# A small first transfer, constants made later, turned copies on VectorE, and a new order on all engines

## The reference

```python
x = x + tanh(g_xattn[0]) * _L0_xattn_ref(_layernorm(x), ctx, ctx, mask, ...)   # A0: 16 heads of 8, softmax attention
x = x + tanh(g_ffn[0])   * _L0_ffn_ref(_layernorm(x), ...)                     # M0: 8 experts (top 2) and 2 shared
x = x + tanh(g_xattn[1]) * _L1_xattn_ref(_layernorm(x), ctx, ctx, mask1, ...)  # A1: 16 heads of 8, with biases
x = x + tanh(g_ffn[1])   * _L1_ffn_ref(_layernorm(x), ...)                     # SW: switched attention, 16 heads of 64
x = x + tanh(g_xattn[2]) * _L2_xattn_ref(_layernorm(x), ctx, ctx, ...)         # ML: mLSTM, 4 heads of 32
x = x + tanh(g_ffn[2])   * _L2_ffn_ref(_layernorm(x), ...)                     # CF: quantised layers around a convolution
x = x + tanh(g_xattn[3]) * _L3_xattn_ref(_layernorm(x), ctx, ctx, ...)         # WA: one head of 128, then a feed-forward
x = x + tanh(g_ffn[3])   * _L3_ffn_ref(_layernorm(x), ...)                     # M3: 16 experts (top 4) and shared ones
```

## Time and profile before

| | |
|---|---|
| median of 3 runs | 2604.3 us (2591.88 to 2605.58) |
| profiled execution, its own time | 2615.43 us |
| its span in the profile | 2613.4 us |
| mean granted TensorE clock | 0.979 |
| busy: TensorE, VectorE, ScalarE, GpSimd | 2329.8, 1580.6, 1411.8, 143.7 us |

### The profile page before, as it was taken

How to read it: one execution, slowest core, us unless ns; L and a number is a source line. 1 busy time by engine, 2 the same in 40 slices (tenths; PEclk the granted TensorE clock), 3 DMA queues, 4 the chain that set the end, 5 groups by cost and what they waited for, 6 DMA issues and landing times.

```text
span 2613.4 us, 51527 instructions
## 1 busy us (share of the span) xinstructions
PE 2329.8 (89%) x19938; PEld 1626.1 (62%) x19938; DVE 1580.6 (60%) x5307; ACT 1411.8 (54%) x3970; POOL 143.7 (5%) x180
## 2 busy tenths in 40 slices
PE   5999889998899888999899998998989989899887
PEld 2668556675566755667556775567755676565765
DVE  3754666547666376664756647556475565755656
ACT  4376264753647436475365744557345573455734
POOL 0000100001000010000100001000100001000010
PEclk9999999999999899999999999999999999999999
DMA  3024000340004300043000420005200051000510
GB/s 156 1 66 114 9 13 1 80 99 17 5 1 100 80 15 7 1 100 80 17 5 1 111 69 17 5 1 122 58 17 5 1 138 42 19 3 9 137 35 5
DMA packets 312292, 115.19 MB, mean 44 GB/s; under 512 B 268737, under 2 KB 295361, under 8 KB 311793
## 3 DMA queue, kind: packets, MB, share of 16 engines
q1 hardware_dynamic: 312048, 111.90, 17.0%
HBM read 63.64 MB, written 48.23 MB: 43 GB/s over the span
## 4 chain that ended last, share of the span: by engine, by line
PE 52%; DVE 24%; ACT 9%; DMA 7%; issue 4%; POOL 3%; SPq 1%; DVEq 0%; ACTq 0%
PE banks L462 5%; PE banks L406 5%; PE banks L343 5%; ACT PP L820 3%; PE banks L292 3%; DVE nm L1163 2%; PE banks L546 2%; POOL mv L1682 2%; PE banks L340 2%; PE banks L430 2%; PE banks L573 2%; PE banks L679 2%; DMA mix_d<-gs 2%; PE banks L354 2%; DMA o_d<-oa 2%
## 5 line engine op out<-in xcount | busy, mean ns | idle before, releaser
L820 ACT ACTIVATE PP<-banks,nm 128x128 f32<-128x128 f32 x1568 | 450.3, 397 | 171.6 <-DVE nm L1163 117.4
L1163 DVE TENSOR_REDUCE nm<-banks 128x4 f32<-128x512 f32 (+1 forms) x400 | 260.0, 675 | 309.3 <-PE banks L343 263.7
L406 PE MATMUL banks<-w_sb,PP 128*128 128x128 f32 x1536 | 248.2, 285 | 44.4 <-ACT PP L827 24.5
L827 ACT ACTIVATE PP<-banks 128x512 f32<-128x512 f32 (+1 forms) x400 | 242.2, 613 | 63.2 <-PE banks L406 48.3
L292 PE MATMUL banks<-identb 128*128 128x256 bf16 x1632 | 267.4, 288 | 7.2 <-ACT PP L978 4.5
L406 PEld LDWEIGHTS banks<-w_sb,PP 128*128 128x128 f32 x1536 | 166.4, 142 | 138.4 <-ACT PP L827 90.9
L1682 POOL TENSOR_TENSOR mv<-mv,half 128x2 f32<-128x2 f32 x160 | 115.5, 722 | 2278.9 <-DVE mv L1060 2278.9
L292 PEld LDWEIGHTS banks<-identb 128*128 128x128 bf16 x1632 | 161.0, 104 | 68.0 <-issue 26.4
L462 PE MATMUL banks<-w_sb,qk 128*128 128x128 f32 x1280 | 193.4, 287 | 1.3 <-DVE qk L1298 1.3
L462 PEld LDWEIGHTS banks<-w_sb,qk 128*128 128x128 f32 x1280 | 162.9, 191 | 30.3 <-issue 11.4
L811 ACT ACTIVATE xnT<-banks 128x256 f32<-128x256 f32 x128 | 48.8, 381 | 191.0 <-PE banks L300 191.0
(11 more groups left out here) (281 smaller groups left out, 4329.0 us busy)
## 6 DMA issues: line engine op xcount, KB each, us to landing
va<-v_d SPq DMA_DIRECT2D x32, 512.0 KB, 4.1
o_d<-oa SPq DMA_DIRECT2D x64, 256.0 KB, 3.9
va<-o_d SPq DMA_DIRECT2D x32, 512.0 KB, 4.1
pv_d<-PP SPq DMA_DIRECT2D x32, 256.0 KB, 2.1
oa<-pv_d SPq DMA_DIRECT2D x32, 256.0 KB, 3.6
v_d<-PP SPq DMA_DIRECT2D x16, 512.0 KB, 4.6
v_d<-tmp SPq DMA_DIRECT2D x16, 512.0 KB, 5.6
w_sb<-weights SPq DMA_DIRECT2D x1, 5603.0 KB, 23.1
```

Of the source, the lines that this page charges most:

```text
L406: e = pe.transpose(bank(k, 2)[:, cols(j)], P[k][:, 512 * (u % 2) + 128 * j:][:, 0:128], ident)
L820: e = act.activation(P[k][:, 512 * (u % 2) + 128 * j:][:, 0:128], bank_[:, cols(j)], ACT.Exp, bias=nm[k][:, m:m + 1])
L827: act.activation(PT[k][:, 512 * (u % 2):512 * (u % 2) + maps * 128], bank(k, 2)[:, 0:maps * 128], ACT.Copy).then_inc(pT_ok[k], 1)
L1163: e = dve.tensor_reduce(m, b3(scores[:, 0:maps * 128], maps), AX.X, ALU.max, negate=True)
```

## The change

1. The columns of the weights are reordered, so that the identity, `head4`, the gates and A0's four weights come first. They are loaded by a transfer of their own (`s_w0`, 652 columns of 128 partitions, 326 KB) right behind lane 0's x. ScalarE's first instruction and the bf16 identity wait for it alone, and TensorE starts after the identity. The table pick, the mask and the rest of the first weights are issued behind lane 1's context.
2. The other constants are made by `dve_constants`, a generator advanced once after each of the first seven maps of lane 0's first attention. TensorE waits for its end (`s_rows`, 9 steps) before the first output product. The table pick lies in `tmp[0]` and a temporary in `mixd[0]` instead of in `qk[0]`.
3. In A0 and A1 the turned maps are copied by VectorE instead of ScalarE: after the maxima of maps u-1 and u (u odd) come the copies of the same two maps. The other attentions keep their copies on ScalarE.
4. On SyncE, one loop over the two sequences loads the values and stores and loads the mixture gates, where there were two.
5. All beats, TURN, SHIFT and SPARES are new (the lists of beats are left out below).

```diff
-TURN, SHIFT = 36969, 1327
+TURN, SHIFT = 39873, 1339
...
 SPARES = (
-    0, 0, 1, 0, 0, 0, 2, 0, 0, 0, 1, 0, 0, 0, 0, 3, 0, 6, 0, 0, 6, 4, 0, 0, 0, 0, 3, 0, 0, 0, 0, 0, 4, 0, 0, 0, 2, 0, 0, 0,
-    0, 4, 0, 4, 0, 0, 2, 0, 0, 0, 0, 0, 0, 0, 0, 0, 0, 0, 0, 2, 2, 0, 0, 0, 0, 0, 0, 0, 0, 7, 1, 0, 0, 0, 0, 0, 15, 0, 6, 4,
-    0, 0, 10, 0, 2, 1, 0, 0, 0, 2, 3, 0, 0, 2, 0, 0, 0, 0, 3, 0, 0,)
+    0, 0, 3, 0, 0, 2, 0, 0, 0, 0, 0, 3, 0, 1, 0, 0, 0, 1, 0, 0, 0, 0, 3, 0, 1, 1, 3, 0, 0, 0, 0, 0, 0, 5, 0, 0, 0, 0, 0, 0,
+    0, 0, 0, 0, 2, 0, 0, 0, 0, 4, 0, 3, 1, 1, 0, 0, 0, 0, 0, 1, 0, 0, 0, 0, 0, 0, 0, 0, 0, 0, 0, 4, 0, 0, 0, 0, 10, 0, 6, 4,
+    0, 0, 8, 0, 0, 0, 5, 0, 0, 0, 0, 0, 4, 5, 1, 1, 0, 2, 0, 3, 0,)
...
+ROWS_STEPS = 9
...
-        pick_ld = qk[0][0:3 * E3, 0:E3 // 2 * 128]
+        pick_ld = tmp[0][0:3 * E3, 0:E3 // 2 * 128]
...
             pe.wait_ge(xnT_ok[k], xnT_ok.n(i, (XT_O0, XT_O1)[s]))
+            if i + s == 0:
+                pe.wait_ge(s_rows, ROWS_STEPS)
...
                     act_map(act, k, i, 8 * s + u, u, bank(k, u % 2), HQ)
-                if u >= 1:
-                    yield
-                    act_map_turned(act, k, i, 8 * s + u - 1, u - 1, HQ)
...
+            late = dve_constants(dve) if i + k + s == 0 else iter(())
             for u in range(8):
                 yield
                 dve_max(dve, k, i, 8 * s + u, 4 * (u % 4), bank(k, u % 2), HQ, s == 0)
+                if u % 2:
+                    for n in (u - 1, u):
+                        yield
+                        dve.wait_ge(pT_ps[k], pT_ps.n(i, 8 * s + n))
+                        if n >= 2:
+                            dve.wait_ge(o_ps[k], o_ps.n(i, 8 * s + n - 2))
+                        dve.tensor_copy(PT[k][:, cols(n % 2, 512)], bank(k, 2)).then_inc(pT_ok[k], 1)
+                next(late, None)
...
-            dve.wait_ge(s_w1, 48)
-            dve.tensor_copy(identb[:, :], ident)
+            dve.wait_ge(s_w0, 16)
+            dve.tensor_copy(identb[:, :], ident).then_inc(s_setup, 1)
+
+        def dve_constants(dve):
+
+            part = mixd[0][0:67, 0:256].bitcast(BF16)
+            rest = w("rows")[0:67, :]
+            dve.wait_ge(s_w1, 48)
+            dve.tensor_copy(part, rest).then_inc(s_rows, 1)
             dve.tensor_copy(causb[:, :], w("causal"))
...
-            act.wait_ge(s_w1, 48)
+            act.wait_ge(s_w0, 16)
...
                                      pv_d[k][b].rearrange("(g t) (e d) -> (t e) g d", t=16, e=E1)).then_inc(pv_ld[b][k], 16)
-                    for b in range(G):
                         yield
                         sp.wait_ge(mx_ok[k], mx_ok.n(i, b))
...
-            first = COLS["sq1"][0]
+            small, first = COLS["causal"][0], COLS["sq1"][0]
             load_x(0, 0)
+            sp.dma_start(wt[:, 0:small], w_in[:, 0:small]).then_inc(s_w0, 16)
             load_ctx(0, 0)
+            load_x(1, 0)
+            load_ctx(1, 0)
             sp.dma_start(pick_ld, pick_in).then_inc(s_w1, 16)
             sp.dma_start(m1_ld[:, :], mask1_in).then_inc(s_w1, 16)
-            sp.dma_start(wt[:, 0:first], w_in[:, 0:first]).then_inc(s_w1, 16)
-            load_x(1, 0)
-            load_ctx(1, 0)
+            sp.dma_start(wt[:, small:first], w_in[:, small:first]).then_inc(s_w1, 16)
             sp.dma_start(wt[:, first:NCOLS], w_in[:, first:NCOLS]).then_inc(s_w2, 16)
```

36 lines of the change are left out of this document (17 added, 19 removed), and 56 rows, old and new, of tables (BEATS_ACT, BEATS_DVE, BEATS_PE).

## The result

The changed kernel takes 2584.9 us (median of 19 runs, 2574.67 to 2592.63), the kernel before in the same sessions 2598.7 us (19 runs): ratio 0.9944, 95% interval 0.9928 to 0.9960. It is faster by 14 us, about 0.5%, where I had forecast 40. The profiled execution took 2583.45 us. That of before, on which my sum stands, took 2615.4 us and so lies at the upper end of its runs: the two profiles differ by 32 us, the medians by 14. Profiles show places here, and only ratios show sizes.

A forecast was written before the change was run, and what follows sets the result against it. TensorE's stream was taken as the bound. Per turn 1.6 - 0.4 + 3.2 - 0.9 = 3.5 us, 28 us over 8 turns, with the start 40.5 us: 2564 us on the median, range 2525 to 2604 for 8 in 10.

The forecast's parts named there:

- The start: Before lane 0's first attention: first matmul 14.5 us earlier, at about 6.7 us; net gain 12.5 us (7 to 14.5).
- The late constants: Constants made by VectorE in lane 0's first attention, mostly hidden there: price taken as 1 us, between 0 and 6.
- the big transfer: At the start, the first piece of constants waits for the transfer of the remaining first weights: up to 1 us more.
- The copies' price: Small attentions: 256 copies leave ScalarE at 0.623 us each and cost VectorE 0.69 us each, 177 us more there.
- The spares: Matmuls nobody needs: 44 fewer per turn in the small attentions gain 3.2 us; 16 more elsewhere cost 0.9 us.
- The stall that goes: Small attentions: a quarter of TensorE's 6.2 idle us goes, 1.6 us per turn (0 to 5), less 0.4 for copies.
- The order: All stages, new beats: two priced places cancel, so 0 is taken, with 2 us per turn either way.
- my second rival: Attentions and first mixture: VectorE's waiting copies delay the other lane's maxima, the turns gain nothing, 2592 us; chance 0.14.
- the clock falls: Switched attention or small attentions: fewer spares lower TensorE's clock; 2604 us (chance 0.04) or about 2640 (chance 0.07).
- my list of signs: Foreseen: attention windows of 43 to 44 us, other stages within 2 us; wrong if the switched attention onward changes over 3.

The follow-up runs named there:

- a_nostart: The changed kernel with the old start (one first transfer, all constants before TensorE's first instruction): 2602.4 us, ratio 0.9996 to the kernel before.
- b_start: The kernel before with the new start alone (small first transfer, constants made in lane 0's first attention): 2594.75 us, ratio 0.9971.
- b_spares: The kernel before with only the changed kernel's table of spare matmuls: 2640.9 us, ratio 1.0161.
- a_spares: The changed kernel with only the old table of spare matmuls: 2669.5 us, ratio 1.0259 to the kernel before.
- b_copies: The kernel before with the small attentions' turned copies moved to VectorE, old order otherwise: 2727.4 us, ratio 1.0495.
- b_bare_att: The kernel before with all spares of its two small attentions removed, 84 per turn: 2610.3 us, ratio 1.0039.
- h_sw: New start; order, spares and ScalarE copies of the kernel before up to the switched attention, order and spares of the changed kernel from there: 2579.2 us, ratio 0.9918.
- a_bare_att: The changed kernel with all spares of its two small attentions removed, 40 per turn: 2618.0 us, ratio 1.0078 to the kernel before.
- b_act_more: The kernel before with one unneeded ScalarE activation over 128x512 behind each turned copy of turns 2 to 8: 2652.1 us.
- h_a1: New start; first attention and its MLP as in the kernel before, changed kernel's order, spares and VectorE copies from the second attention on: 2630.8 us, ratio 1.0103.
- a_copies_act: The changed kernel with the small attentions' turned copies back on ScalarE at the same places of the order: 2833.7 us, ratio 1.0901 to the kernel before.
- h_warm: h_sw with 22 matmuls on ones before TensorE's first instruction and six more spares at each lane's first eight places: 2575.4 us, ratio 0.9922.

## Why the prediction was wrong

**The start: right.** I put it at 12.5 us (7 to 14.5). It is 14.5 at the first add in either order, 13.5 in the ratios of a_nostart and the changed kernel, and 7.5 (1 to 14) by b_start. First matmul 6.30 (about 7 foreseen), first maximum 17.48 (near 16). The late constants cost nothing that shows: in b_start, where the order is the old one, the first add gains 14.5 us, of 14.7 at the first matmul (6.52). I took 1.0 us for them and up to 1 us for the big transfer.

**The copies' price: right.** 256 copies of 0.689 us; VectorE 1752.9 us (1758 foreseen), ScalarE 1283.2 (1253 foreseen, too low by 30: the durations of ScalarE's instructions, summed over the two traces, fall by 157 us, from 1775.8 to 1618.7, but busy time counts overlapping instructions once and falls by 129; a duration is no busy time where an engine overlaps its instructions). The Trainium skill (VectorE: DVE Perf Modes, section on the TRN2 errata) gives 120 + 512 cycles, an estimate of 0.66 us; the trace has 0.689.

**The spares: the step that failed.** I took two thirds of them to lie on the chain at 0.108 us each, 3.2 us per turn and by far the largest term of the turns. That came from the chain's share of line 292. But a spare in front of a wait stands on the chain too: where it is taken out, the wait behind it takes its place. With all 84 gone the old attentions shrank by 0.8 and 0.0 us, where the term gives 3 us each, and the kernel was slower. Where the clock stayed at the upper level they shrank by 0.9 and 0.6, a sixth of the spares' time; at that share the 44 spares of the term would have been worth 0.8 us per turn, not 3.2. Their absence has a price besides. In these bare kernels the lower level appears in attentions that had none (up to 44.4 us in one A0), and the tables in the wrong order, where both the number and the places are off, cost 1.6% (b_spares) and 3.2% (a_spares).

**The stall that goes: failed as well.** 1.6 us per turn was a quarter of the idle time in the attentions, and no row sized it. I read the 24.5 us of the earlier trace rows as these attentions' wait for copies; 18.6 of them are the switched attention's. Only 5.9 us of the run, 0.7 per turn, could go from the turning matmuls, and they did not: the wait is 8.1 us now, and the one for exponentials rose from 13.9 to 27.9, since the maxima come later from a VectorE with more to do. A0 is the same as before, M0 and A1 are 1.2 and 1.3 us longer (means of both lanes).

**The order: not zero, but two terms that cancel.** M0, A1 and the pair WA and M3 lose 3.2 us per turn, and ML and CF, where no copy moved, gain 5.3. Part of that gain is an accident of one execution: the profile of before spent 12.0 us per turn in ML and CF at the lower level, the changed kernel 5.8. Executions of the old order with 4.6 and 5.7 us there (b_copies, b_bare_att) have ML and CF at 52.9 and 53.2 us, those of the new order with 4.6 to 5.8 (a_nostart, h_sw, a_bare_att, the changed kernel) at 49.7 to 50.5: order and table together are worth about 3 us there. (The mLSTM stage has ten spares per turn fewer in the new table, 1.1 us at most.) At the first attention the new order costs 6.6 us, once, by the clock. And the one turn that I cut was the longest of its run, so the idle time that I read outside the attentions was high for a turn.

Taken together, order, copies and spares are worth 0.9996 (0.9970 to 1.0022), nothing that can be measured, and the start makes the result. That is the outcome of my second rival (the turns gain nothing, only the start is left, 2592), to which I gave 0.14. Its mechanism is part of the answer: VectorE delays exponentials. Its price is not shown alone. The rival "the clock falls" did not happen inside the changed kernel's attentions, which ran at 1.00, but it is part of what happened to most of the kernels that took a part of the change, and I had it down as a side case. Of my list of signs three spoke against me: the windows did not shrink although the spares did, ML and CF moved by more than 2 us each, and the switched attention and what follows changed by more than 3 us a turn (5.5 less).

**What the clock explains.** Of the kernels that lose over 1%, all but b_act_more have more time at the lower level than the kernel before and the changed one, b_spares only little more. At the start the clock explains the new order's loss in full: from the first matmul to the first add the changed kernel takes 55.2 us with 31.2 at the lower level, the kernel before 48.2 with 17.1. That is 7.0 us longer for 14.1 us more. The Trainium skill (TensorE: Matmul & The Clock Gate, HAM oscillation) prices time at the lower level at half its length. By it the 14.1 us would be 7.0, an estimate that the traces bear out here. Within one execution the same stage in the same order gives a price too, and it is lower: lane 0's A0 of a_bare_att takes 47.4 us with none, 51.9 with 10.2 and 64.2 with 44.4, and that of b_copies 51.1 with none, 54.8 with 10.2 and 57.9 with 17.1, so 0.36 to 0.44 us for each. Part of the loss may fall into waits that TensorE has anyhow; that was not tested. By the page's half the 13.1 us of h_a1 would be 6.6 us, where A1 grew by 5.0 over the changed kernel and M0 by 3.6 over the kernel before, each in its own order; the 55.1 of a_copies_act would be 27.6, where A0 to A1 grew by 32.8. By this count the clock is the larger part of these two losses, and a part is there without it.

**What stays open.** Why the new order gains 3 us in ML and CF was not taken apart piece by piece. What the copies on VectorE cost or give inside the new order is not known, for the only kernel that moved them alone there, a_copies_act, also ran 55.1 us per turn at the lower level. Why the clock falls at one wait and not at another is open too. Nor do these runs show whether h_sw or h_warm beats the changed kernel: 0.9918 and 0.9922 against 0.9944, with intervals that overlap.

## What to carry to other kernels

Work that stands on the chain is not thereby a cost: ask what would end the wait if it were gone, and try it with the whole group removed before its share of the chain goes into a sum. Where an order was laid out as a whole, its parts (places of copies, spare counts, seams) can't be exchanged one by one, and a part that loses alone says little about the whole; so cut such a change into what is outside the order, which adds up (here the start), and what is inside, which doesn't. Compare stage lengths only between executions with a like share at the lower clock level, or between passes of one execution. And give a wait to a stage before a term is taken from it: a helper's line can serve several.

## What the runs showed of the hardware that I had not expected

- The granted clock went to 0.50 behind waits of 1.4 to 2.2 us (h_a1, the changed kernel's start, a_nostart), and stayed there for up to 27.3 us with TensorE busy 23.7 of them. Such a wait alone doesn't decide it: in the trace of the changed kernel 30 waits of 1.2 us and more began at the upper level, and 14 of them had a fall of the clock in the 7 us that I counted behind each; 9 of its 22 stretches at the lower level had no wait of over 0.2 us in the 7 us ahead of them.
- Every kernel here starts at the lower level, and how long it stays there differs with the order and the spares: 17.1 us from the first matmul in the kernel before, 3.9 in the changed one (which then fell back), 37.3 in a_bare_att. The profile's windows print 1.00 there, since the records begin later; two equal matmuls take 1.03 us ahead of the first record and 0.60 behind it.
- A TensorE that is busy 38 of 40 us can be at a mean clock of 0.57 (a_bare_att). The same 311 matmuls of one stage kept it busy 93% of 64.2 us at a mean clock of 0.65 and 86% of 47.4 us at 1.00, so the busy share alone doesn't show the loss.
- Behind a window with ten fewer matmuls whose result nobody reads, the next stage ran at 0.80 instead of 1.00 (a_spares: 32.5 us against 28.1).
- Over the run ScalarE's instructions overlap each other by 364 us in the kernel before (1775.8 summed, 1411.8 busy).
